# Splitting the left operand of a CIN layer: one VectorE subtraction over 128 partitions instead of ScalarE's rounding plus a subtraction over 64

## The chip, the core and the metric

The kernel runs on one core of a Trainium2 chip. The metric is device time in microseconds (us) of one execution. The core's engines run side by side, each through its own instruction stream: TensorE (PE; its weight loads are listed as PEld), VectorE (DVE), ScalarE (ACT), GpSimd (POOL) and SyncE (SP, which here only starts DMAs). They wait for each other on semaphores.

## What is computed

A recommendation tower: 32 embedding rows of 64 elements are gathered for each of 1024 batch rows, a two-layer CIN (pairwise products of the fields, mixed by a weight matrix, ReLU, summed over the 64 elements) turns them into 192 features, and a small MLP gives one number per batch row. Cut to the part that matters:

```python
x0 = h = e                                  # (1024, 32, 64)
for W, b in ((W0, b0), (W1, b1)):           # W0: 128 x 1024, W1: 128 x 2048
    z = einsum('bhd,bmd->bhmd', h, x0).reshape(batch, H * 32, 64)
    out = relu(einsum('bcd,oc->bod', z, W) + b[None, :, None])
    # layer 0: the first 64 outputs become h, the other 64 are features; layer 1: all are features
z = sum(features, axis=-1)
y = relu(relu(concat(z, dense) @ W_top1 + b_top1) @ W_top2 + b_top2) @ W_top3
```

## The kernel before

**Tiling.** A block is 16 batch rows (1024 columns of batch row x element); there are 64 blocks. Each has two halves of 512 columns, so there are 128 steps `m`, half `b = m % 2`. An "odd step" has b = 1, an "even step" b = 0. The loop body has four steps (`BODY = 4`), the first and the last body are written out. Each engine's order is written by hand in its own `step` function, and nothing reorders it.

**Layer 0** uses the symmetry of the products. VectorE multiplies `xr` (the field values, in PSUM) by `rot_low` (the fields rotated over the partitions, reloaded by DMA) into `prod[0]` (L500). TensorE multiplies its four 512-column parts in fp32 with `w0_sb` into `out0` (L618). What is left over, the products of a field with the one 16 places further, is the "left" operand. It is made once per block: ScalarE copies `left_x` into `lz` in PSUM (L364, `copy_left`), VectorE multiplies it in place by `left_y` (L506, `left_products`), and the product is split into a rounded high part and the low rest, so that one fp32r matmul (L620) does in place of an fp32 one. The 128 partitions of `lz` hold the products repeated: partitions 0 to 63 of `left_parts` are to hold the rounded product, and 64 to 127 the product less its rounded value. Matmul L620 multiplies `left_parts` by `w0l_parts` and closes the group of `out0`.

**Layer 1.** ScalarE writes ReLU(`out0`) repeated over the partitions into `hrep[0]` and `hrep[1]` (L389). VectorE multiplies these by `rot_low` and `rot_high` into `prod[1]` (L550), `z4` (L557, L571), `prod[2]` (L562) and `prod[3]` (L568). Each product is split: ScalarE rounds it into `zh` (L376), and the rest `zl` is made by GpSimd for the three large tiles (L221) and by VectorE for `z4` (L517). TensorE runs three fp32r matmuls for each 512-column part of it (L636: `w1h` x `zh`, `w1l` x `zh`, `w1h` x `zl`), and multiplies the remaining parts of `prod[3]` whole, in fp32 (L626). ScalarE adds the bias and applies ReLU (L382, L406), and VectorE sums once per block (L521).

**Order around the change.** VectorE's odd step m = 2n - 1 goes: L500, L517, L506 (left product of block n), L550, L510 (`left_low`), L557, L562, L517, L568, L571. ScalarE rounds the left product (L370, `round_left`) at the end of its even step, after `hrep[1]` and ahead of L406. TensorE's step goes: the three splits of step m - 1, layer 0 of step m + 1 (L618, L620), the splits 3 and 0 of step m, and the whole part (L626).

Of the kernel before, what the change touches and what calls it, by code (L numbers as in the profile page):

```python
# [5 lines left out]
F32 = mybir.dt.float32  # L6
F32R = mybir.dt.float32r
I32 = mybir.dt.int32
ALU = mybir.AluOpType
ACT = mybir.ActivationFunctionType  # L10
AX = mybir.AxisListType

P = 128
BATCH, FIELDS, DIM, DENSE = 1024, 32, 64, 16
OUT = 128
HID = OUT // 2
# [9 lines left out]
SC = COLS // HALVES  # L26
# [12 lines left out]
LOW = ROTS // 2  # L39
# [33 lines left out]
def cin_mlp(nc, ids, first_row, tables, dense_t, w0_first, w0_second, w0l_first, w0l_second, w1, b0, b1,  # L73
            w_top1, b_top1, w_top2, b_top2, w_top3, y):
    ctx = ExitStack()
    with ctx:
        def sb(name, shape, dt=F32):
            return ctx.enter_context(nc.sbuf_tensor(name, shape, dt))

        def pb(name, shape):  # L80
            return ctx.enter_context(nc.psum_tensor(name, shape, F32))

        def sem(name):
            return ctx.enter_context(nc.semaphore(name))
# [11 lines left out]
        prod = [sb(f"prod{k}", [P, LOW, SC]) for k in range(4)]  # L96
        zh = [sb(f"zh{u}", [P, SIZES[u], SC], F32R) for u in range(PARTS)]
        zl = [sb(f"zl{u}", [P, SIZES[u], SC], F32R) for u in range(PARTS)]
        left_x = sb("left_x", [P, SC])
        left_y = sb("left_y", [P, SC])  # L100
        left_parts = sb("left_parts", [P, SC], F32R)
        relu = sb("relu", [P, 1 + HALVES, SC])

        w0_sb = sb("w0_sb", [P, LOW, OUT])
        w0b_sb = sb("w0b_sb", [P, LOW, OUT])
        w0l_sb = sb("w0l_sb", [P, HALVES, OUT])
        w0lb_sb = sb("w0lb_sb", [P, HALVES, OUT])
        w0l_parts = sb("w0l_parts", [P, HALVES, OUT], F32R)
# [21 lines left out]
        lz = pb("lz", [P, SC])  # L130
# [33 lines left out]
        l0_done = sem("l0_done")  # L164
# [4 lines left out]
        sums_made = sem("sums_made")  # L169
        left_copied = sem("left_copied")  # L170
        left_made = sem("left_made")
        left_rounded = sem("left_rounded")
        left_split = sem("left_split")
        feat0_made = sem("feat0_made")
# [12 lines left out]
        def known(i):  # L187
            return isinstance(i, int)
# [162 lines left out]
        def _(act):  # L351
# [14 lines left out]
            def round_left(n):  # L366
                act.wait_ge(left_made, n + 1)
                if not known(n) or n > 0:
                    act.wait_ge(l0_done, n * 2)
                act.activation(left_parts[:, :], lz[:, :], ACT.Copy).then_inc(left_rounded, 1)  # L370

            def round_split(m, u, size, made, product):
                act.wait_ge(made, m + 1)
# [35 lines left out]
            def step(i, c):  # L409
                m = i * BODY + c  # L410
                b = c % HALVES
                if is_up_to(i, c, LAST - 2):
                    copy_x(m + 2, b)
                if b == 0 and is_up_to(i, c, LAST - 2):
                    copy_left(i * 2 + (c + 2) // 2)
                round_split(m, 0, in_parts(0, b), p1_made, prod[1])
                round_split(m, 3, in_parts(3, b), z4_made[0], z4)
                if is_past(i, c, 0):
                    finish_l1(m - 1, 1 - b, i * 2 + (c + 1) // 2 - 1)
                round_split(m, 1, in_parts(1, b), p2_made, prod[2])  # L420
                if is_up_to(i, c, LAST - 1):
                    replicate_h0(m + 1)
                round_split(m, 2, in_parts(2, b), p3_made, prod[3])
                round_split(m, 4, in_parts(4, b), z4_made[1], z4)
                if is_up_to(i, c, LAST - 1):
                    replicate_h1(m + 1)
                if b == 0 and is_up_to(i, c, LAST - 2):
                    round_left(i * 2 + (c + 2) // 2)
                if is_up_to(i, c, LAST - 1):
                    finish_l0(m + 1, 1 - b, i * 2 + (c + 1) // 2)  # L430
# [16 lines left out]
            copy_left(0)  # L447
            copy_x(1, 1)
            round_left(0)
            replicate_h0(0)  # L450
            finish_l0(0, 0, 0)
# [38 lines left out]
        def _(dve):  # L490
# [16 lines left out]

            def left_low(n):
                dve.wait_ge(left_rounded, n + 1)
                nc.vector.tensor_tensor(left_parts[HID:P, :], lz[HID:P, :], left_parts[HID:P, :].bitcast(F32),  # L510
                                        ALU.subtract).then_inc(left_split, 1)

            def low_part4(m, k):
# [13 lines left out]
            def sum_block(n):  # L527
                dve.wait_ge(relu0_made, n * HALVES + 1)
                if known(n) and n == 0:
                    sum_rows(0, slice(0, HID), slice(0, 1))  # L530
                else:
                    dve.wait_ge(relu1_made, n * HALVES)
                    sum_rows(n, slice(0, P), slice(0, 1 + HALVES))

            def step(i, c):
# [16 lines left out]
                if b == 1 and is_up_to(i, c, LAST - 1):  # L552
                    left_low(i * 2 + (c + 1) // 2)
# [19 lines left out]
                if b == 0:  # L573
                    sum_block(i * 2 + c // 2)

            nc.vector.memset(feat0[:, :], 0.0).then_inc(zeroed, 1)
            dve.wait_ge(w0_loaded, 64)

# [14 lines left out]
            products_l0(0, 0, 1)  # L593
            left_products(0)
            left_low(0)
            for c in range(BODY):
                step(0, c)
# [156 lines left out]
```

## Time and profile before

| | before |
|---|---|
| three timed runs, us | 2001.33, 2001.28, 1998.69 (median 2001.28) |
| the profiled execution, us | 2000.27 |
| span of its trace, first to last instruction, us | 1998.4 |
| PE / PEld busy in the span | 98% / 67% |
| DVE / ACT / POOL busy in the span | 96% / 86% / 90% |
| DMA, mean rate | 182 GB/s |
| granted TensorE clock, mean | 0.997 of full speed |

"Busy" is the sum of the instructions' own durations, as a share of the span. Where an instruction is recorded as starting before the one ahead of it on the same engine has ended, the two overlap, and the busy share of a stretch counts the common time once. A start-to-start distance ("pitch") therefore tells more than a duration. "issue" as a releaser means that the view shows nothing that the engine waited for.

### The profile page before, as it was taken

What the parts mean: (1) busy time and instruction counts of PE and PEld (TensorE: products, weight loads), DVE (VectorE), ACT (ScalarE), POOL (GpSimd) and SP (SyncE); (2) the same over time, 40 slices, a digit from 0 to 9 for tenths busy, and PEclk for the clock granted to TensorE, in tenths of its full rate; (3) what the DMA queues carried; (4) which work ended last, traced back from release to release, by engine and by line L of the source; (5) the groups of instructions that cost most, each with busy time, mean ns of one, the idle gap of its engine ahead of it and who ended that gap; (6) DMA issues with size and microseconds to landing.
All of it is one profiled execution on the core that took longest, in us unless ns stands there. A gap on an engine that the chain in (4) does not pass through costs nothing.

```text
span 1998.4 us, 28527 instructions
## 1 busy us (share of the span) xinstructions
PE 1951.9 (98%) x7176; PEld 1342.8 (67%) x7176; DVE 1913.1 (96%) x1230; ACT 1711.2 (86%) x1943; POOL 1804.2 (90%) x708
## 2 busy tenths in 40 slices
PE   2999999999999999999999999999999999999998
PEld 1677677667666666666666766776776676676664
DVE  3999999999999999999999999999999999999991
ACT  2889898888889889889889888888888888888883
POOL 3999999999999999999999999999999999999881
PEclk9999999999999999999999999999999999999999
DMA  7988888888788888788788788888888887887820
GB/s 190 216 209 194 185 188 195 183 189 193 183 190 193 182 191 195 178 193 194 179 194 192 182 193 190 185 193 186 188 193 183 190 194 180 192 194 179 192 67 0
DMA packets 268304, 364.13 MB, mean 182 GB/s; under 512 B 107505, under 2 KB 107889, under 8 KB 268162
## 3 DMA queue, kind: packets, MB, share of 16 engines
q1 hardware_dynamic: 258338, 352.61, 77.0%
q0 software_dynamic: 8192, 8.40, 1.7%
q10 hardware_dynamic: 1760, 2.96, 0.5%
q8 instruction: 6, 0.10, 0.0%
q14 instruction: 8, 0.07, 0.0%
HBM read 347.02 MB, written 16.78 MB: 182 GB/s over the span
## 4 chain that ended last, share of the span: by engine, by line
PE 91%; POOL 5%; issue 2%; SPq 1%; DMA 1%; ACT 0%; DVE 0%; POOLq 0%
PE out L636 60%; PE out L618 20%; PE out L626 8%; POOL zl L221 4%; PE out L620 1%; SPq L263 0%; PE out L683 0%; DMA fields_dram<-emb 0%; POOL emb L204 0%; PE hrep L683 0%; SPq L288 0%; SPq L273 0%; PE out L676 0%; PE z L676 0%; PE hrep L676 0%
## 5 line engine op out<-in xcount | busy, mean ns | idle before, releaser
L221 POOL TENSOR_TENSOR zl<-prod,zh 128x2048 fp32r<-128x2048 f32 (+2 forms) x384 | 1545.6, 4055 | 68.8 <-ACT zh L376 51.5
L636 PE MATMUL out<-zh,w1h 128*128 128x512 f32 x1856 | 757.2, 408 | 5.5 <-DVE zl L517 3.9
L636 PE MATMUL out<-zl,w1h 128*128 128x512 f32 x1856 | 725.5, 391 | 0.0
L636 PE MATMUL out<-zh,w1l 128*128 128x512 f32 x1856 | 724.6, 390 | 0.0
L376 ACT ACTIVATE zh<-prod 128x2048 fp32r<-128x2048 f32 (+2 forms) x384 | 652.5, 1699 | 69.3 <-DVE prod L562 44.4
L389 ACT ACTIVATE hrep<-out,b_sb 32x512 f32<-32x512 f32 (+1 forms) x768 | 495.2, 645 | 90.7 <-PE out L620 80.9
L618 PE MATMUL out<-prod,w_sb 128*128 128x512 f32 x1024 | 465.3, 597 | 35.0 <-DVE prod L500 30.1
L636 PEld LDWEIGHTS out<-zh,w1h 128*128 128x128 f32 x1856 | 348.8, 188 | 174.1 <-POOL zl L221 61.0
L636 PEld LDWEIGHTS out<-zh,w1l 128*128 128x128 f32 x1856 | 349.4, 188 | 75.9 <-issue 3.5
L636 PEld LDWEIGHTS out<-zl,w1h 128*128 128x128 f32 x1856 | 349.0, 188 | 76.1
L618 PEld LDWEIGHTS out<-prod,w_sb 128*128 128x128 f32 x1024 | 195.3, 191 | 232.5 <-issue 222.7
L517 DVE TENSOR_TENSOR zl<-z,zh 128x1024 fp32r<-128x1024 f32 x256 | 311.0, 1215 | 8.8 <-ACT zh L376 8.8
L500 DVE TENSOR_TENSOR prod<-xr,rot_low 128x2048 f32<-128x2048 f32 x128 | 292.0, 2281 | 19.4 <-DMA rot_low<-fields_dram 14.6
L204 POOL DMA_INDIRECT emb<-in_tables,idx x256 | 245.1, 957 | 59.1 <-issue 46.6
L562 DVE TENSOR_TENSOR prod<-hrep,rot_high 128x2048 f32<-128x2048 f32 x128 | 292.6, 2286 | 2.0
L568 DVE TENSOR_TENSOR prod<-hrep,rot_high 128x2048 f32<-128x2048 f32 x128 | 292.0, 2281 | 0.0
L550 DVE TENSOR_TENSOR prod<-hrep,rot_low 128x2048 f32<-128x2048 f32 x128 | 292.0, 2281 | 0.0
L376 ACT ACTIVATE zh<-z 128x1024 fp32r<-128x1024 f32 x256 | 261.6, 1022 | 10.7
L626 PE MATMUL out<-prod,w_sb 128*128 128x512 f32 x384 | 185.5, 591 | 0.0
L557 DVE TENSOR_TENSOR z<-hrep,rot_low 128x1024 f32<-128x1024 f32 x128 | 157.2, 1228 | 2.1
L571 DVE TENSOR_TENSOR z<-hrep,rot_low 128x1024 f32<-128x1024 f32 x128 | 156.5, 1223 | 0.0
L521 DVE TENSOR_REDUCE sums<-relu 128x1536 f32 (+2 forms) x66 | 112.4, 1703 | 7.0 <-ACT relu L382 7.0
(61 smaller groups left out, 696.2 us busy)
## 6 DMA issues: line engine op xcount, KB each, us to landing
rot_low<-fields_dram SPq DMA_DIRECT2D x512, 256.0 KB
rot_high<-fields_dram SPq DMA_DIRECT2D x512, 256.0 KB
xrep<-fields_dram SPq DMA_DIRECT2D x256, 128.0 KB
fields_dram<-emb SPq DMA_DIRECT2D x512, 32.0 KB, 5.2
left_x<-fields_dram SPq DMA_DIRECT2D x256, 64.0 KB, 2.4
left_y<-fields_dram SPq DMA_DIRECT2D x256, 64.0 KB, 2.2
emb<-in_tables,idx POOLq DMA_INDIRECT x256
w_sb<-in_w ACTq DMA_DIRECT2D x1, 1024.0 KB
```

Of the source, the lines that this page charges most:

```text
L204: pool.indirect_dma_start(out=emb[b][:, g, :], out_offset=None, in_=tables, in_offset=bass.IndirectOffsetOnAxis(ap=idx[b][:, g:g + 1], axi ...
L221: pool.tensor_tensor(zl[u][:, 0:size, :], product[:, 0:size, :], zh[u][:, 0:size, :].bitcast(F32), ALU.subtract).then_inc(zl_made[u], 1)
L376: act.activation(zh[u][:, 0:size, :], product[:, 0:size, :], ACT.Copy).then_inc(zh_made[u], 1)
L389: op = act.activation(hrep[j][to, :], out0[h, :], ACT.Relu, bias=b0_sb[h, :])
L500: nc.vector.tensor_tensor(prod[0][:, :, :], repeated(xr, LOW), rot_low[c][:, :, :], ALU.mult).then_inc(x_made, 1)
L517: nc.vector.tensor_tensor(zl[3 + k][:, :, :], z4[:, :, :], zh[3 + k][:, :, :].bitcast(F32), ALU.subtract).then_inc(zl_made[3 + k], 1)
L550: nc.vector.tensor_tensor(prod[1][:, :, :], repeated(hrep[0], LOW), low[:, :, :], ALU.mult).then_inc(p1_made, 1)
L562: nc.vector.tensor_tensor(prod[2][:, :, :], repeated(hrep[0], LOW), high[:, :, :], ALU.mult).then_inc(p2_made, 1)
L568: nc.vector.tensor_tensor(prod[3][:, :, :], repeated(hrep[1], LOW), high[:, :, :], ALU.mult).then_inc(p3_made, 1)
L618: nc.tensor.matmul(out0[:, :], w0_sb[:, t, :], prod[0][:, t, :], start=t == 0, stop=False)
L626: mm = nc.tensor.matmul(out1[:, :], w1_sb[:, tiles(P3, t, t + 1).start, :], prod[3][:, t, :], start=False, stop=False)
L636: mm = nc.tensor.matmul(out1[:, :], w[:, k, :], z[:, t, :], start=start and t == 0 and part == 0, stop=stop and t == size - 1 and part == 2)
```

## The change

A new tile `left_high` takes ScalarE's rounded product, on partitions 64 to 127 only; its partitions 0 to 63 are set to zero once, at the start. VectorE then writes all 128 partitions of `left_parts` as `lz - left_high`: on the upper half of the tile (0 to 63) that is the product less zero, rounded as it is written to fp32r, and on 64 to 127 the product less its rounded value. ScalarE's rounding waits for `left_split` of the block before in place of `l0_done`, and VectorE's subtraction waits for `l0_done` (the last reader of `left_parts`) as well as for ScalarE. To make room, the second half of the layer-0 weights is loaded into `prod[3]` at the start, and not into a tile of its own.

```diff
-        w0b_sb = sb("w0b_sb", [P, LOW, OUT])
+        left_high = sb("left_high", [P, SC], F32R)
+        w0b_sb = prod[3][:, 0, :].rearrange("p (a b) -> p a b", b=OUT)
...
             def round_left(n):
                 act.wait_ge(left_made, n + 1)
                 if not known(n) or n > 0:
-                    act.wait_ge(l0_done, n * 2)
-                act.activation(left_parts[:, :], lz[:, :], ACT.Copy).then_inc(left_rounded, 1)
+                    act.wait_ge(left_split, n)
+                act.activation(left_high[HID:P, :], lz[HID:P, :], ACT.Copy).then_inc(left_rounded, 1)
...
             def left_low(n):
                 dve.wait_ge(left_rounded, n + 1)
-                nc.vector.tensor_tensor(left_parts[HID:P, :], lz[HID:P, :], left_parts[HID:P, :].bitcast(F32),
+                if known(n) and n == 0:
+                    dve.wait_ge(left_zeroed, 1)
+                else:
+                    dve.wait_ge(l0_done, n * 2)
+                nc.vector.tensor_tensor(left_parts[:, :], lz[:, :], left_high[:, :].bitcast(F32),
                                         ALU.subtract).then_inc(left_split, 1)
...
+            nc.vector.memset(left_high[0:HID, :].bitcast(F32), 0.0).then_inc(left_zeroed, 1)
             nc.vector.memset(feat0[:, :], 0.0).then_inc(zeroed, 1)
```

VectorE in the first odd step inside the loop, before. A name in brackets is a semaphore that the instruction waits for, and `REGISTER_ALU` is an instruction of the engine's sequencer that computes a wait's value and may itself carry a wait:

```order
L505 REGISTER_ALU [waits left_copied]
L506 TENSOR_TENSOR lz<-lz,left_y 128x512 [waits left_y_loaded]
L550 TENSOR_TENSOR prod<-hrep,rot_low 128x2048 [waits zl_made0,hrep0_made]
L510 TENSOR_TENSOR left_parts<-lz,left_parts 64x512 [waits left_rounded]
L557 TENSOR_TENSOR z<-hrep,rot_low 128x1024 [waits zl_made4,hrep1_made]
L562 TENSOR_TENSOR prod<-hrep,rot_high 128x2048 [waits zl_made1,rot_high_loaded1]
```

The same place of the changed kernel (its line numbers are six or so higher):

```order
L507 REGISTER_ALU [waits left_copied]
L508 TENSOR_TENSOR lz<-lz,left_y 128x512 [waits left_y_loaded]
L556 TENSOR_TENSOR prod<-hrep,rot_low 128x2048 [waits zl_made0,hrep0_made]
L515 REGISTER_ALU [waits left_rounded]
L516 TENSOR_TENSOR left_parts<-lz,left_high 128x512 [waits l0_done]
L563 TENSOR_TENSOR z<-hrep,rot_low 128x1024 [waits zl_made4,hrep1_made]
L568 TENSOR_TENSOR prod<-hrep,rot_high 128x2048 [waits zl_made1,rot_high_loaded1]
```

No instruction moves. The subtraction covers 128 partitions in place of 64, its wait for ScalarE sits on a register instruction ahead of it, and it waits for `l0_done` itself.

ScalarE at the end of an even step in the loop, before:

```order
L389 ACTIVATE hrep<-out,b_sb 32x512 x3
L369 REGISTER_ALU [waits left_made]
L370 ACTIVATE left_parts<-lz 128x512 [waits l0_done]
L406 ACTIVATE relu<-out,b_sb 64x512 [waits sums_made]
L357 REGISTER_ALU
L358 ACTIVATE xr<-xrep 128x512 [waits x_made]
```

And now:

```order
L391 ACTIVATE hrep<-out,b_sb 32x512 x3
L372 ACTIVATE left_high<-lz 64x512 [waits left_split,left_made]
L408 ACTIVATE relu<-out,b_sb 64x512 [waits sums_made]
L359 REGISTER_ALU
L360 ACTIVATE xr<-xrep 128x512 [waits x_made]
```

Again nothing moves: the register instruction is gone, and the rounding covers 64 partitions. TensorE's, GpSimd's and SyncE's streams are the same in both kernels.

## Rows read from the trace of the kernel before

**Rows 1.** The page: busy time by engine, and the chain that ended last by line

```profile
PE 1951.9 (98%) x7176; PEld 1342.8 (67%) x7176; DVE 1913.1 (96%) x1230; ACT 1711.2 (86%) x1943; POOL 1804.2 (90%) x708
...
PE out L636 60%; PE out L618 20%; PE out L626 8%; POOL zl L221 4%; PE out L620 1%; SPq L263 0%; PE out L683 0%; DMA fields_dram<-emb 0%; POOL emb L204 0%; PE hrep L683 0%; SPq L288 0%; SPq L273 0%; PE out L676 0%; PE z L676 0%; PE hrep L676 0%
```

**Rows 2.** Busy time of each engine, 100 to 1900 us

```profile
100.00:1900.00 1800.00, 1800.00 (x6695) 1249.99 (x6694) 1794.36 (x1145) 1597.84 (x1811) 1693.63 (x657) 1.00 0.83 189
```

**Rows 3.** VectorE, odd step: start us, duration us, engine, line, what

```profile
418.23 1.22 DVE L517 TENSOR_TENSOR zl<-z,zh 128x1024 fp32r<-128x1024 f32 x1
419.36 0.69 DVE L506 TENSOR_TENSOR lz<-lz,left_y 128x512 f32<-128x512 f32 x1
419.96 2.28 DVE L550 TENSOR_TENSOR prod<-hrep,rot_low 128x2048 f32<-128x2048 f32 x1
422.27 0.69 DVE L510 TENSOR_TENSOR left_parts<-lz,left_parts 64x512 fp32r<-64x512 f32 x1
423.00 1.23 DVE L557 TENSOR_TENSOR z<-hrep,rot_low 128x1024 f32<-128x1024 f32 x1
424.26 2.29 DVE L562 TENSOR_TENSOR prod<-hrep,rot_high 128x2048 f32<-128x2048 f32 x1
```

**Rows 4.** VectorE, the even step behind it

```profile
434.26 2.28 DVE L550 TENSOR_TENSOR prod<-hrep,rot_low 128x2048 f32<-128x2048 f32 x1
436.46 1.22 DVE L557 TENSOR_TENSOR z<-hrep,rot_low 128x1024 f32<-128x1024 f32 x1
437.59 2.28 DVE L562 TENSOR_TENSOR prod<-hrep,rot_high 128x2048 f32<-128x2048 f32 x1
```

**Rows 5.** VectorE at the kernel's start, the narrow weight additions

```profile
5.75 0.28 DVE L580 TENSOR_TENSOR w_sb<-w_sb,w0b_sb 32x128 f32<-32x128 f32 x1 [3.80 <-DMA w0lb_sb<-in_w0l_second]
6.06 0.29 DVE L580 TENSOR_TENSOR w_sb<-w_sb,w0b_sb 64x128 f32<-64x128 f32 x1
6.38 0.56 DVE L580 TENSOR_TENSOR w_sb<-w_sb,w0b_sb 128x384 f32<-128x384 f32 x1
6.86 0.42 DVE L582 TENSOR_TENSOR w0l_sb<-w0l_sb,w0lb_sb 128x256 f32<-128x256 f32 x1
```

**Rows 6.** All L510 from 93 us on: count, durations (ns), first and last start

```profile
L510 DVE TENSOR_TENSOR left_parts<-lz,left_parts x62: 694/695/696, 93.7 to 1915.9; 64x512 fp32r<-64x512 f32 x62
```

**Rows 7.** TensorE's weight loads (PEld) in one block, in order of time

```profile
427.18 0.19 PEld L620 LDWEIGHTS out<-left_parts,w0l_parts 128*128 128x128 f32 x1 [0.24 <-issue]
...
427.91 0.19 PEld L636 LDWEIGHTS out<-zh,w1l 128*128 128x128 f32 x1
...
431.77 0.41 PEld L626 LDWEIGHTS out<-prod,w_sb 128*128 128x128 f32 x2
...
433.72 0.19 PEld L636 LDWEIGHTS out<-zh,w1l 128*128 128x128 f32 x1
...
441.77 0.19 PEld L618 LDWEIGHTS out<-prod,w_sb 128*128 128x128 f32 x1 [0.24 <-issue]
442.20 0.19 PEld L620 LDWEIGHTS out<-left_parts,w0l_parts 128*128 128x128 f32 x1 [0.24 <-issue]
...
442.86 0.19 PEld L636 LDWEIGHTS out<-zh,w1l 128*128 128x128 f32 x1
...
446.73 0.41 PEld L626 LDWEIGHTS out<-prod,w_sb 128*128 128x128 f32 x2
447.78 0.19 PEld L636 LDWEIGHTS out<-zh,w1h 128*128 128x128 f32 x1 [0.64 <-POOL zl L221]
447.88 0.19 PEld L636 LDWEIGHTS out<-zh,w1l 128*128 128x128 f32 x1
```

**Rows 8.** ScalarE: the left rounding, and the first rounding of the even step

```profile
420.17 0.60 ACT L370 ACTIVATE left_parts<-lz 128x512 fp32r<-128x512 f32 x1 [0.67 <-DVE lz L506]
...
436.58 1.92 ACT L376 ACTIVATE zh<-prod 128x2048 fp32r<-128x2048 f32 x1
```

**Rows 9.** GpSimd's subtractions of the even step

```profile
438.58 12.62 POOL L221 TENSOR_TENSOR zl<-prod,zh 128x2048 fp32r<-128x2048 f32 x3 [0.44 <-issue]
```

More of the change, by code:

```diff
@@ L171, in cin_mlp @@
         left_made = sem("left_made")
+        left_zeroed = sem("left_zeroed")
         left_rounded = sem("left_rounded")
```

## Prediction

> **What bounds the kernel now.** I read the page first. It points at TensorE: 98% busy against VectorE's 96%, and its matmuls fill nearly all of the chain that ended last, with some per cent of GpSimd's subtraction in it [rows 1]. Those two shares are too near to each other to choose by, so I looked at the steady stretch alone. From 100 to 1900 us TensorE is busy for 1800.00 of 1800 us, VectorE for 1794.36, ScalarE for 1597.84, GpSimd for 1693.63 [rows 2]. TensorE's figure proves little, since the modelled ends of its matmuls overlap the next starts and cover any short wait. VectorE's ends are recorded, so its 5.64 missing microseconds can be looked for.
>
> That is done in the timeline of VectorE, by comparing each start with the end of the instruction ahead. Normally the next one starts before the one ahead has ended: L506 at 419.36, while L517 ran from 418.23 for 1.22 us, to 419.45. That is 0.09 early, and so it is at L550 in the same rows. Around L510 it is otherwise. L550 ends at 422.24 and L510 starts at 422.27; L510 ends at 422.96 and L557 starts at 423.00; L557 ends at 424.23 and L562 starts at 424.26 [rows 3]. These are three transitions that are 0.03 to 0.04 late in place of 0.08 to 0.09 early. No other place in a block has that, and none has a wait: VectorE never idles for anybody. So in the steady stretch VectorE sets the pace, with not one instruction waiting, though the page's chain names TensorE. The visible idle time (60 blocks x 3 x 0.03 = 5.4 us, nearly all of the 5.64) is only the smaller part of what these transitions cost.
>
> The pace is very even: the 62 starts of L510 from 93.7 to 1915.9 us give 1822.2 / 61 = 29.87 us for each block [rows 6].
>
> **Why those three.** L510 is the one instruction in the loop on 64 partitions, starting at partition 64; all the others on VectorE start at 0. The start of the kernel shows the same around narrow additions: the one on partitions 32 to 63 ends at 6.03 and the next, on 64 to 127, starts at 6.06; that ends at 6.35 and the one on all 128 starts at 6.38; but that one would end at 6.94, and the next, which starts at partition 0 as well, starts at 6.86 [rows 5]. So the late transitions go with a change of the first partition, and neither with a wait nor with the shape of the 128-partition ones. The third one around L510 fits as well, if reads and writes count by themselves: L510 wrote to SBUF from partition 64, L557 writes to PSUM, and L562 is the next that writes to SBUF.
> The Trainium skill has this as a rule ("VectorE: DVE Perf Modes", § Two Vector instructions with no wait between them): an instruction is held until all earlier ones have finished if its first input from SBUF or PSUM, or its output there, starts in another group of 32 partitions than the last one did. By that rule, exactly these three are held; the trace agrees.
>
> **What the change removes.** After it, the subtraction starts at partition 0 with all its operands, as its neighbours do. Its duration should stay: 0.69 us with 64 partitions, as with the 128 of L506 [rows 3]. By pitches:
> - L550 to the next start: 2.31 (419.96 to 422.27) becomes 2.20, as in the even step (434.26 to 436.46) [rows 3, 4]: 0.11.
> - The subtraction itself: 0.73 (422.27 to 423.00) becomes the 0.60 of L506 (419.36 to 419.96) [rows 3]: 0.13.
> - L557: 1.26 (423.00 to 424.26) becomes 1.13 (436.46 to 437.59) [rows 3, 4]: 0.13.
>
> Together 0.37 us for each block on VectorE, or 61 x 0.37 = 22.6 us if nothing else bound.
>
> **What TensorE leaves of it.** TensorE is the next bound, and very near, so its real waits in a block must be found. I take them from its weight loads, whose records are not modelled [rows 7].
> - From the load of L620 to the second load behind it: 0.73 in the odd step (427.18 to 427.91), 0.66 in the even one (442.20 to 442.86). Behind L620 stands split 3, which waits for VectorE's L517; in the odd step that comes shortly after the late transitions. Wait: 0.07.
> - From the first load of L626 to the second load of the split behind: 1.95 where it has four matmuls (431.77 to 433.72), 1.15 where it has two (446.73 to 447.88). Two fp32 matmuls are 2 x 0.43 (441.77 to 442.20), so 1.09 is due. Wait: 0.06, for GpSimd. GpSimd's start at 438.58 follows the end of ScalarE's rounding at 438.50, and that started at 436.58 behind the end of VectorE's L550 at 436.54 [rows 4, 8, 9]. VectorE sets this one too.
>
> So TensorE can run a block in 29.87 - 0.13 = 29.74 us, and VectorE in 29.50. The lesser gain counts: 61 x 0.13 = **7.9 us**. Then TensorE never waits, and VectorE idles some 0.24 us in each block for it.
> The Trainium skill ("Perfetto Trace Analysis", § Identifying the Most-Contended Engine) says that matmul busy time misjudges TensorE's headroom and that the share of the weight loads should be used. That share is 1249.99 / 1800 = 69% here, which would leave room for VectorE's whole 22.6 us; I trust the pitches, since the loads stand back to back with fp32 matmuls that last longer than a load.
>
> **The rest of the change at nothing.** The zeroing is one short instruction ahead of 3.80 us of idle time for the weights [rows 5]; it would cost something only beyond that. The weights' second half in `prod[3]` is read before L568 first writes there. ScalarE's rounding waits for a semaphore it waited for already in L364. VectorE's new wait for `l0_done` is one that `hrep0_made`, awaited by L550 just ahead, implies. The wait for ScalarE is as before: its rounding ends at 420.77, 1.50 us before L510 starts [rows 3, 8]. If that cover were gone, what is queued behind is L557, and ScalarE's rounding of `z4`. GpSimd's idle time of 0.44 in an even step [rows 9] is more than the 0.13 by which it must go faster. Nothing outside the 61 blocks changes: at the start and the end others are waited for.
>
> **The sum.** The profiled execution took 2000.27 us, 1.0 less than the median of 2001.28. 2000.27 - 7.9 = 1992.4; set against the median, 1993.4. I take 1993.
>
> **Rivals.**
> - *TensorE has more room* (10%): its matmuls are a little slower behind a wait and recover, or the pitches hide waits. Bound above by VectorE: 2001.3 - 22.6 = 1978.7; half-way, 1987. For it: the weight loads' share above. Against it: the even-step places show no wait at all.
> - *Another chain binds first* (17%). ScalarE feeds GpSimd .08 us before its start [rows 8, 9]. If most of the 0.44 is GpSimd's own issue time, only 0.02 to 0.06 a block is gained: 1 to 4 us, 1997 to 2000.
> - *The late transitions have another cause* (13%), as the fp32r output, or the rounding waited for. Then they stay, and so does the time: 2001.3. Against it: the kernel's start, which has them with neither.
> - *Slower* (5%): the new register instruction carries the wait for ScalarE, and the sequencer may hand the subtraction over late. Nearest price: the 0.44 that GpSimd idles under "issue" [rows 9]. Less the 0.37 regained, VectorE would take 0.07 more a block, 2001.3 + 4.3 = 2005.6. It decides from 0.37 on. Against it: L506 has such a register instruction with a wait ahead of it, and starts 0.09 early [rows 3].
>
> The forecast itself has 55%; its own range is 1989 to 1997.
>
> **Numbers.** About 0.2% (4 us) is what a measurement of this kernel can tell from no change. Faster by more: the forecast (nearly all of it), the first rival, and half of the second: 0.75. Within: the rest of the second, the third: 0.21. Slower: 0.04. The range reaches from the middle of the first rival, with a little beyond, to the upper end of the second: 1985 to 2000.
>
> **What would show it.** VectorE's transitions around the subtraction 0.08 to 0.09 early, with pitches of 2.20, 0.60 and 1.13; idle time of some 0.24 us a block on VectorE, which has none now; blocks of 29.74 us; 0.66 from L620's load to the second behind it in odd steps too. Wrong would be: transitions still late (the cause is not the first partition), early ones with an unchanged 29.87 (VectorE was not the pace), or blocks near 29.50 (TensorE's bound misjudged).

## The result and the profile after

The changed kernel takes 1992.97 us in the median of 7 runs (1990.08 to 1994.51), the kernel before 2000.71 in the median of 7 (1998.15 to 2001.37). The ratio is 0.9964, 95% interval 0.9953 to 0.9976, or 7.2 us less by the ratio (7.7 by the medians).

| | before | after |
|---|---|---|
| the profiled execution, us | 2000.27 | 1994.51 |
| span of its trace, us | 1998.4 | 1992.6 |
| PE / DVE busy in the span | 98% / 96% | 98% / 95% |

The page of the changed kernel tells a reader next to nothing. Busy times by engine, and the chain that ended last by line:

```profile
PE 1944.8 (98%) x7176; PEld 1352.0 (68%) x7176; DVE 1900.6 (95%) x1231; ACT 1708.0 (86%) x1943; POOL 1803.5 (91%) x708
...
PE out L645 60%; PE out L627 21%; PE out L635 8%; POOL zl L223 4%; PE out L629 1%; SPq L265 0%; DMA fields_dram<-emb 0%; PE out L692 0%; POOL emb L206 0%; PE hrep L692 0%; SPq L290 0%; PE out L685 0%; SPq L275 0%; PE z L685 0%; PE hrep L685 0%
```

These shares are those of [rows 1] to within one per cent, though another engine now sets the pace. ScalarE's rounding is still there: on 64 partitions it takes 0.60 us, as it did on 128. VectorE's timeline in an odd step does show it (start us, duration us, engine, line; L516 is the subtraction):

```profile
447.45 0.69 DVE L508 TENSOR_TENSOR lz<-lz,left_y 128x512 f32<-128x512 f32 x1
448.05 2.28 DVE L556 TENSOR_TENSOR prod<-hrep,rot_low 128x2048 f32<-128x2048 f32 x1
450.25 0.68 DVE L516 TENSOR_TENSOR left_parts<-lz,left_high 128x512 fp32r<-128x512 f32 x1
450.85 1.22 DVE L563 TENSOR_TENSOR z<-hrep,rot_low 128x1024 f32<-128x1024 f32 x1
451.98 2.28 DVE L568 TENSOR_TENSOR prod<-hrep,rot_high 128x2048 f32<-128x2048 f32 x1
```

L556 would end at 450.33, and L516 starts at 450.25; the two starts behind it are 0.08 and 0.09 before the end of the one ahead. The pitches are 2.20, 0.60 and 1.13, where [rows 3] have 2.31, 0.73 and 1.26. All subtractions from 93 us on:

```profile
L516 DVE TENSOR_TENSOR left_parts<-lz,left_high x62: 675/678/681, 93.4 to 1907.5; 128x512 fp32r<-128x512 f32 x62
```

(1907.5 - 93.4) / 61 = 29.74 us for a block, against 29.87 before [rows 6]. VectorE now has a wait, in the even step of each block:

```profile
435.56 2.28 DVE L568 TENSOR_TENSOR prod<-hrep,rot_high 128x2048 f32<-128x2048 f32 x1
438.00 1.23 DVE L523 TENSOR_TENSOR zl<-z,zh 128x1024 fp32r<-128x1024 f32 x1 [0.17 <-ACT zh L378]
```

L568 ends at 437.84 and the next one starts 0.16 later, where it would start 0.08 before: 0.24 us in all. The view of waits from 93 to 1910 us has 59 of these, 9.7 us together, and no other wait on VectorE. TensorE's weight loads (PEld), the places of [rows 7] in the changed kernel:

```profile
426.51 0.19 PEld L629 LDWEIGHTS out<-left_parts,w0l_parts 128*128 128x128 f32 x1 [0.24 <-issue]
...
427.17 0.19 PEld L645 LDWEIGHTS out<-zh,w1l 128*128 128x128 f32 x1
...
441.47 0.19 PEld L629 LDWEIGHTS out<-left_parts,w0l_parts 128*128 128x128 f32 x1 [0.24 <-issue]
...
442.13 0.19 PEld L645 LDWEIGHTS out<-zh,w1l 128*128 128x128 f32 x1
...
446.00 0.41 PEld L635 LDWEIGHTS out<-prod,w_sb 128*128 128x128 f32 x2
446.65 0.19 PEld L645 LDWEIGHTS out<-zh,w1h 128*128 128x128 f32 x1 [0.24 <-issue]
447.08 0.19 PEld L645 LDWEIGHTS out<-zh,w1l 128*128 128x128 f32 x1 [0.24 <-issue]
```

From L629 to the second load behind it there are now 0.66 in both steps, and from L635 1.08 in place of 1.15. In the view of waits of the weight loads, 93 to 1910 us, the kernel before has 115 for GpSimd's L221; the changed kernel has none for any engine. So TensorE is the one that sets 29.74, which the experiments on the pace test.

### The profile page after: what moved, and what is told of

Same layout as the page of the kernel before. It is cut to its first block, busy times and chain, and to the rows that moved or that the text cites. A ratio compares the mean times of both kernels' runs of the same rounds, so it can differ in the third digit from the quotient of the medians.

```text
span 1992.6 us, 28592 instructions
## 1 busy us (share of the span) xinstructions
PE 1944.8 (98%) x7176; PEld 1352.0 (68%) x7176; DVE 1900.6 (95%) x1231; ACT 1708.0 (86%) x1943; POOL 1803.5 (91%) x708
## 4 chain that ended last, share of the span: by engine, by line
PE 91%; POOL 4%; issue 2%; SPq 1%; DMA 1%; ACT 0%; DVE 0%; POOLq 0%
PE out L645 60%; PE out L627 21%; PE out L635 8%; POOL zl L223 4%; PE out L629 1%; SPq L265 0%; DMA fields_dram<-emb 0%; PE out L692 0%; POOL emb L206 0%; PE hrep L692 0%; SPq L290 0%; PE out L685 0%; SPq L275 0%; PE z L685 0%; PE hrep L685 0%
## 5 line engine op out<-in xcount | busy, mean ns | idle before, releaser
L645 PE MATMUL out<-zh,w1h 128*128 128x512 f32 x1856 | 777.3, 419 | 6.8 <-DVE zl L523 5.7
L556 DVE TENSOR_TENSOR prod<-hrep,rot_low 128x2048 f32<-128x2048 f32 x128 | 291.6, 2278 | 0.0
L568 DVE TENSOR_TENSOR prod<-hrep,rot_high 128x2048 f32<-128x2048 f32 x128 | 291.5, 2277 | 0.0
L635 PE MATMUL out<-prod,w_sb 128*128 128x512 f32 x384 | 185.4, 591 | 0.0
L384 ACT ACTIVATE relu<-out,b_sb 128x512 f32<-128x512 f32 x128 | 87.9, 687 | 51.8 <-PE out L645 51.8
```

The costliest lines, as they stand in the source:

```text
L556: nc.vector.tensor_tensor(prod[1][:, :, :], repeated(hrep[0], LOW), low[:, :, :], ALU.mult).then_inc(p1_made, 1)
L568: nc.vector.tensor_tensor(prod[2][:, :, :], repeated(hrep[0], LOW), high[:, :, :], ALU.mult).then_inc(p2_made, 1)
L635: mm = nc.tensor.matmul(out1[:, :], w1_sb[:, tiles(P3, t, t + 1).start, :], prod[3][:, t, :], start=False, stop=False)
L645: mm = nc.tensor.matmul(out1[:, :], w[:, k, :], z[:, t, :], start=start and t == 0 and part == 0, stop=stop and t == size - 1 and part == 2)
```

## Experiments: what makes a transition late

**The other half.** In the kernel before, the narrow subtraction is put on partitions 0 to 63. The four products of high and low parts are then formed in another order, and nothing else changes.

```diff
-                nc.vector.tensor_tensor(left_parts[HID:P, :], lz[HID:P, :], left_parts[HID:P, :].bitcast(F32),
+                nc.vector.tensor_tensor(left_parts[0:HID, :], lz[0:HID, :], left_parts[0:HID, :].bitcast(F32),
                                         ALU.subtract).then_inc(left_split, 1)
```

> The kernel before with one edit: the narrow subtraction works on partitions 0 to 63 of left_parts and lz in place of 64 to 127, still in place, still 64 partitions wide, still behind ScalarE's rounding of all 128. (The four products of high and low parts are the same ones, with the halves exchanged.) If a transition is late because the first partition changes: the three transitions around L510 are 0.08 to 0.09 us early as everywhere else, pitches 2.20, 0.60, 1.13, a block takes 29.74 us and the kernel some 7 us less than before (ratio 0.9964, as with the change). If it is the width of 64 partitions, the in-place operand, or the wait for ScalarE's rounding that makes them late: late as before (2.31, 0.73, 1.26), 29.87 us a block, ratio 1.000.

Measured: 1992.98 us, ratio to before 0.9969 (0.9958 to 0.9979). VectorE's timeline, and all of its L510:

```profile
924.26 2.28 DVE L550 TENSOR_TENSOR prod<-hrep,rot_low 128x2048 f32<-128x2048 f32 x1
926.46 0.68 DVE L510 TENSOR_TENSOR left_parts<-lz,left_parts 64x512 fp32r<-64x512 f32 x1
927.06 1.22 DVE L557 TENSOR_TENSOR z<-hrep,rot_low 128x1024 f32<-128x1024 f32 x1
928.19 2.28 DVE L562 TENSOR_TENSOR prod<-hrep,rot_high 128x2048 f32<-128x2048 f32 x1
```

```profile
L510 DVE TENSOR_TENSOR left_parts<-lz,left_parts x62: 672/676/680, 93.7 to 1907.9; 64x512 fp32r<-64x512 f32 x62
```

Still 64 partitions, still in place, still behind ScalarE, and yet all three transitions are early and a block takes 29.74 us. The width was not the cause; the first partition was. This one-line edit gains what the whole change gains (0.9969 against 0.9964, with intervals that overlap).

**The change without its width.** In the changed kernel, the subtraction covers only partitions 64 to 127, and `left_parts` 0 to 63 is zeroed once. The product's high part is left out of the sum.

```diff
-                nc.vector.tensor_tensor(left_parts[:, :], lz[:, :], left_high[:, :].bitcast(F32),
+                nc.vector.tensor_tensor(left_parts[HID:P, :], lz[HID:P, :], left_high[HID:P, :].bitcast(F32),
...
-            nc.vector.memset(left_high[0:HID, :].bitcast(F32), 0.0).then_inc(left_zeroed, 1)
+            nc.vector.memset(left_parts[0:HID, :].bitcast(F32), 0.0).then_inc(left_zeroed, 1)
```

> The changed kernel (new tile, new semaphores, weights' second half in prod[3]) but with the subtraction on partitions 64 to 127 alone; left_parts 0 to 63 is zeroed once, so the product's high part is left out of the sum. If the first partition decides: three late transitions again, pitches 2.31, 0.73, 1.26, 29.87 us a block, ratio to before 1.000, so nothing else in the change has a price or a gain. If another part of the change brought the time (the tiles' places, the removed register instruction on ScalarE, the operand that is no longer in place): 29.74 us a block, ratio 0.9964.

Measured: 1999.84 us, ratio 1.0002 (0.9993 to 1.0011).

```profile
926.48 2.29 DVE L556 TENSOR_TENSOR prod<-hrep,rot_low 128x2048 f32<-128x2048 f32 x1
928.80 0.69 DVE L516 TENSOR_TENSOR left_parts<-lz,left_high 64x512 fp32r<-64x512 f32 x1
929.53 1.23 DVE L563 TENSOR_TENSOR z<-hrep,rot_low 128x1024 f32<-128x1024 f32 x1
930.79 2.29 DVE L568 TENSOR_TENSOR prod<-hrep,rot_high 128x2048 f32<-128x2048 f32 x1
```

The three late transitions are back (2.32, 0.73, 1.26), without an operand in place. So is the time. The tiles' places, the semaphores and the register instructions of the change, taken together, have neither a price nor a gain outside that interval, which is -1.4 to 2.2 us.

**One place later.** In the kernel before, the narrow subtraction stands behind L557.

```diff
-                if b == 1 and is_up_to(i, c, LAST - 1):
-                    left_low(i * 2 + (c + 1) // 2)
...
                 nc.vector.tensor_tensor(z4[:, :, :], repeated(hrep[1], 2), low[:, 0:2, :],
                                         ALU.mult).then_inc(z4_made[0], 1)
+                if b == 1 and is_up_to(i, c, LAST - 1):
+                    left_low(i * 2 + (c + 1) // 2)
```

> The kernel before with the narrow subtraction (partitions 64 to 127) one place later, behind L557 and ahead of L562. If a transition is late because the last access to the same memory (SBUF or PSUM, reads and writes apart) started at another partition: L557 to the subtraction and the subtraction to L562 are late, but L562 to L517 is early, since L562 itself sets all of it back; two late transitions in place of three, 0.12 less on VectorE, 29.75 us a block, some 6 to 7 us less than before. If a narrow instruction makes the next two late whatever they access: three late transitions and 29.87 us, ratio 1.000.

Measured: 1992.13 us, ratio 0.9965 (0.9951 to 0.9978). The product into `z4` is L555 here:

```profile
925.58 1.23 DVE L555 TENSOR_TENSOR z<-hrep,rot_low 128x1024 f32<-128x1024 f32 x1
926.84 0.70 DVE L510 TENSOR_TENSOR left_parts<-lz,left_parts 64x512 fp32r<-64x512 f32 x1
927.57 2.29 DVE L562 TENSOR_TENSOR prod<-hrep,rot_high 128x2048 f32<-128x2048 f32 x1
929.78 1.22 DVE L517 TENSOR_TENSOR zl<-z,zh 128x1024 fp32r<-128x1024 f32 x1
```

```profile
L510 DVE TENSOR_TENSOR left_parts<-lz,left_parts x62: 694/694/697, 93.7 to 1908.6; 64x512 fp32r<-64x512 f32 x62
```

Two transitions are late (926.84 and 927.57, 0.03 each), and the one after is early (929.78 against an end at 929.86). A block takes 29.75 us. So the third one of the kernel before is no after-effect of the narrow instruction as such: it comes because L557, which writes to PSUM, stands between two that write to SBUF. With L562 next, reads and writes are back at partition 0 at once. Moving one line down brings the same time as the change (0.9965 against 0.9964). On VectorE it saves only some 0.12 us a block, but TensorE lets through no more than 0.13 anyway.

## Experiments: who sets the pace

Both kernels lose one of TensorE's matmuls in each step, which is left out of the sum:

```diff
-                    for part, (w, z) in enumerate(((w1h, zh[u]), (w1l, zh[u]), (w1h, zl[u]))):
+                    for part, (w, z) in enumerate(((w1h, zh[u]), (w1l, zh[u]), (w1h, zl[u]))[:2 if u == 1 and t == 2 else 3]):
```

> The kernel before without one fp32r matmul in each step (in split 1, the third part's weights x low product; it is left out of the sum), so TensorE has 2 x 0.227 = 0.45 us less to do in a block and could run one in 29.74 - 0.45 = 29.29 us. VectorE's work is untouched. If VectorE sets the pace of the kernel before at 29.87 us a block, with the holds in it: 29.87 still, and the kernel within some 2 us of before. If TensorE sets it, as the chain of the page has it: 29.4 us a block and 28 us less.

Measured: 1999.72 us, ratio 1.0001 (0.9992 to 1.0011).

```profile
L510 DVE TENSOR_TENSOR left_parts<-lz,left_parts x62: 694/695/697, 92.9 to 1915.2; 64x512 fp32r<-64x512 f32 x62
```

> The changed kernel without the same matmul in each step. If the change took 0.37 us a block from VectorE and TensorE's own pace of 29.74 us hid two thirds of it: now 29.50 us a block, VectorE with no wait again, some 22 us less than before (ratio 0.989). If the change took only the 0.13 from VectorE: 29.74 us, as the changed kernel, ratio 0.996. If some other chain (GpSimd, ScalarE) binds between: a value between the two.

Measured: 1976.15 us, ratio 0.9882 (0.9867 to 0.9897). Its subtractions, and busy times from 300 to 1800 us (PE, PEld, DVE, ACT, POOL):

```profile
L516 DVE TENSOR_TENSOR left_parts<-lz,left_high x62: 679/690/698, 92.9 to 1891.6; 128x512 fp32r<-128x512 f32 x62
```

```profile
300.00:1800.00 1500.00, 1500.00 (x5544) 1029.90 (x5543) 1500.00 (x966) 1348.08 (x1527) 1433.72 (x560) 1.00 0.84 191
```

Taking 128 matmuls (some 29 us of TensorE's time, at the 0.227 us from one fp32r load to the next) out of the kernel before gains nothing: 1822.3 / 61 = 29.87 us a block. That kernel is VectorE's, whatever its page's chain says. Out of the changed kernel the same edit gains some 16 us more (0.9882 against 0.9964): 1798.7 / 61 = 29.49 us a block, with VectorE busy for 1500.00 of 1500 us. So the change took 29.87 - 29.49 = 0.38 us a block from VectorE, and TensorE's own 29.74 hides 0.25 of it. No chain of ScalarE or GpSimd binds down to 29.49.

## Experiments: the clock ahead of the MLP

The changed kernel's trace holds something that the trace of the kernel before does not. TensorE stands idle for 2.52 us behind the last block, for the feature sums; about 1 us after it starts again, its weight loads take 0.34 us in place of 0.19 and follow each other at 0.85 in place of 0.43:

```profile
1955.48 0.30 PEld L685 LDWEIGHTS out<-feat,wt_sb 128*128 128x128 f32 x2 [2.52 <-issue]
1956.02 0.19 PEld L685 LDWEIGHTS out<-sums,wt_sb 128*128 128x128 f32 x1 [0.24 <-issue]
1956.49 0.34 PEld L685 LDWEIGHTS out<-sums,wt_sb 128*128 128x128 f32 x1 [0.28 <-issue]
1957.34 0.34 PEld L685 LDWEIGHTS out<-feat,wt_sb 128*128 128x128 f32 x1 [0.52 <-issue]
1958.20 0.34 PEld L685 LDWEIGHTS out<-feat,wt_sb 128*128 128x128 f32 x1 [0.52 <-issue]
```

The window view of the changed kernel, behind the busy times, has a granted clock of 0.50 there, the lower of the two levels (1.2 of 2.4 GHz):

```profile
1956.50:1959.50 3.00, 3.00 (x5) 1.34 (x4) 0.00 (x0) 0.69 (x1) 0.00 (x0) 0.50 0.00 0
```

The kernel before has 1.00 at that place:

```profile
1964.00:1967.00 3.00, 3.00 (x9) 1.33 (x8) 0.00 (x0) 1.02 (x2) 0.00 (x0) 1.00 0.00 0
```

Four loads at 0.85 in place of 0.43 cost some 1.7 us. So I filled the idle stretch of the changed kernel with matmuls that nobody reads:

```diff
+            for _ in range(11):
+                nc.tensor.matmul(xr[:, :], w1h[:, 0, :], zh[0][:, 0, :], start=True, stop=True)
             pe.wait_ge(top_loaded, 96)
             pe.wait_ge(feat0_made, 2)
```

> The changed kernel with 11 fp32r matmuls whose result nobody reads, put on TensorE behind the last block and ahead of the wait for the feature sums, where it stands idle for some 2.5 us and where the profile of the changed kernel shows a granted clock of 0.50 just afterwards, for some 2.5 us (the profile of before shows 1.00 there). If the clock fell because of the idle stretch: granted clock 1.00 all through the MLP, the two kinds of execution (with and without the fall) come together, and the profiled execution is 1.7 us shorter than that of the changed kernel; the median gains 0 to 1.7 us. If the fall has nothing to do with it: a stretch at 0.50 turns up again, and no gain.

Measured: 1991.62 us, ratio to before 0.9959 (0.9946 to 0.9973). The granted clock stays at 1.00:

```profile
1954.00:1960.00 6.00, 6.00 (x17) 3.00 (x16) 0.52 (x1) 1.37 (x2) 0.00 (x0) 1.00 0.00 0
```

The filler was then put into the one-line version, beside the changed kernel once more, unaltered.

> The kernel before with the narrow subtraction on partitions 0 to 63 (as in e1_low_half) and the 11 matmuls that nobody reads ahead of the MLP. If the two gains are independent and both real: 29.74 us a block, granted clock 1.00 through the MLP, 1991 to 1992 us, ratio to before 0.996. If the filler costs time where the clock would not have fallen: 1993 us or more.

Measured: 1991.88 us, ratio 0.9959 (0.9945 to 0.9972), with 1.00 through the MLP again.

> The changed kernel unaltered, on the same chip as e7_low_filler. Expected ratio to before 0.9964, blocks of 29.74 us. If the fall of the clock ahead of the MLP belongs to this kernel: again a stretch at 0.50. If it comes by chance in any kernel: present or absent.

Measured: 1991.64 us, ratio 0.9963 (0.9949 to 0.9976). Its trace spans 1988.4 us, and the clock did not fall:

```profile
1954.00:1957.00 3.00, 3.00 (x9) 1.33 (x8) 0.00 (x0) 0.95 (x2) 0.00 (x0) 1.00 0.00 0
```

The same kernel has the fall in one execution and not in another, and the fall does not belong to the change. e4_before_less, which is the kernel before less some matmuls, has it too:

```profile
1961.72 0.30 PEld L676 LDWEIGHTS out<-feat,wt_sb 128*128 128x128 f32 x2 [2.52 <-issue]
1963.25 0.34 PEld L676 LDWEIGHTS out<-feat,wt_sb 128*128 128x128 f32 x1 [0.38 <-issue]
```

All eight traces without the filler have the same 2.52 us of idle time. Five of them show the loads at 0.85 shortly behind it (the changed kernel's first trace, e2_upper_half, e3_later, e4_before_less and e5_after_less), and three do not (before, e1_low_half, e8_after_again). So the idle time alone does not decide. With the idle stretch filled, two executions out of two were without the fall; against five of eight, that is too few to call the idle stretch the cause. A gain from the filler is not shown: the medians with it (1991.62, 1991.88) and that of the changed kernel beside e7 (1991.64) are the same.

## Why the prediction was right, point by point

**VectorE set the pace.** Right, and shown by removing TensorE's work from both kernels: 29.87 us a block stayed 29.87 in the kernel before, and 29.74 became 29.49 in the changed one.

**The three late transitions come from the first partition.** Right. The one-line edit on the other half, the changed kernel brought back to partition 64, and the line moved down separate it from width, the operand in place, ScalarE's wait and an after-effect of the narrow instruction. The Trainium skill's rule for held instructions ("VectorE: DVE Perf Modes", § Two Vector instructions with no wait between them) names three late transitions a block in the kernel before, e2_upper_half and e4_before_less, two in e3_later and none in the others; the traces agree in each.

**0.37 us a block on VectorE.** Measured 0.38 where nothing else binds.

**TensorE leaves 0.13 of it.** Right: 29.74 us a block, as worked out from the two waits, and VectorE's new idle time of 0.24. The rival that TensorE has more room, for which the Trainium skill's rule on the share of weight loads spoke ("Perfetto Trace Analysis", § Identifying the Most-Contended Engine), is out. The share over the stretch of [rows 2] went only from 69% to 70% (1263.20 of 1800 us), and TensorE has no wait left:

```profile
100.00:1900.00 1800.00, 1800.00 (x6719) 1263.20 (x6718) 1790.05 (x1151) 1600.68 (x1816) 1699.20 (x659) 1.00 0.83 190
```

The pitches between weight loads told its headroom, their busy share did not.

**61 blocks.** This term was too large; it should have been some 54. TensorE does not wait in the first blocks of the kernel before. Its load of L620 in an odd step and the second load behind it, early and later:

```profile
99.56 0.19 PEld L620 LDWEIGHTS out<-left_parts,w0l_parts 128*128 128x128 f32 x1 [0.24 <-issue]
...
218.52 0.19 PEld L620 LDWEIGHTS out<-left_parts,w0l_parts 128*128 128x128 f32 x1 [0.24 <-issue]
...
219.18 0.19 PEld L636 LDWEIGHTS out<-zh,w1l 128*128 128x128 f32 x1
...
307.70 0.19 PEld L620 LDWEIGHTS out<-left_parts,w0l_parts 128*128 128x128 f32 x1 [0.24 <-issue]
...
308.42 0.19 PEld L636 LDWEIGHTS out<-zh,w1l 128*128 128x128 f32 x1
...
1935.87 0.19 PEld L620 LDWEIGHTS out<-left_parts,w0l_parts 128*128 128x128 f32 x1 [0.24 <-issue]
```

The distance is 0.66 at 218.52 and 0.72 at 307.70. From 99.56 to 307.70 are seven blocks, of 29.73 us each: in the kernel before, too, TensorE first ran at its own pace. VectorE enters the steady stretch ahead of TensorE, loses 0.13 us a block, and only after some seven blocks is it so late that TensorE waits. Where TensorE has less to do (e4_before_less), it catches up sooner: there the distance is 0.66 at 98.31, 0.79 at 127.59 and 0.96 at 157.29. The same two loads in the changed kernel:

```profile
99.37 0.19 PEld L629 LDWEIGHTS out<-left_parts,w0l_parts 128*128 128x128 f32 x1 [0.24 <-issue]
...
1928.47 0.19 PEld L629 LDWEIGHTS out<-left_parts,w0l_parts 128*128 128x128 f32 x1 [0.24 <-issue]
```

At the last step TensorE is 1935.87 - 1928.47 = 7.4 us ahead of where it was. Of this, 0.2 is the start, where the kernel before has this load at 99.56. The gain in the blocks is thus 7.2 us, some 54 blocks of 0.13. The pitch of L510 was 29.87 from the start, so counting VectorE's blocks hid this; TensorE's had to be counted.

**The sum.** 7.9 us were forecast, 7.2 measured by the ratio. The ratio's interval is 4.8 to 9.4 us and holds both, so the timed runs cannot tell 61 blocks from 54; only the loads above do, and that the ratio came out at the same 7.2 is in part luck. The profiled execution gained 5.8 only, since it lost 1.6 of the 7.4 behind the last block, where its clock fell. The other trace of the same kernel spans 4.2 less: some 2.5 from its start (its load at 96.89 in place of 99.37) and 1.7 from the clock. A single pair of profiled executions could not have decided on 0.4%; the block's pitch, which agrees to 0.01 us in all traces, does.

**The rest at nothing.** Right, within the -1.4 to 2.2 us of e2_upper_half.

**A slip in the first rival.** Half-way between 1978.7 and 1993.4 is 1986, not 1987; nothing hangs on it.

## What to carry to other kernels

Compare each start with the end of the instruction ahead on the engine that never waits: a transition that is 0.03 us late where others are 0.08 early costs 0.12 us, and neither busy shares nor a list of waits shows more than a quarter of it. Let all operands of VectorE's instructions start at the same partition as their neighbours' do. If one must be narrow, give it the first partitions: there it had no late transition (e1_low_half). From partition 64 it had two and not three where the next instruction reads and writes the same memories as it does (e3_later). And when an engine's own pace is improved, work out the next engine's pace from gaps between records that are not modelled, and count only the blocks in which that engine really waited.

## What the runs showed that I had not expected

- VectorE's lead over TensorE acts as a store: with 0.13 us lost a block it lasted until about 300 us, and until then the slower engine costs nothing.
- Behind 2.52 us of idle time ahead of the MLP, TensorE's clock fell to 0.50 for some 3 us in five of eight profiled executions, of kernels with and without the change, and stayed at 1.00 in three. That is 1.7 us, a quarter of the change's gain, so single profiled executions of these kernels compare badly.
- A 64-partition subtraction lasts 0.69 to 0.70 us starting at partition 64 and 0.67 to 0.68 starting at 0, with the same elements in each partition. What makes the difference is open: in e5_after_less the 128-partition one, starting at 0, lasts 0.68 to 0.70.
